# Routing for groups of batches, gates in the token table, the expert bias by matmul, a narrower maximum pass

## What is computed

```python
def _L0_ffn_ref(x, wg, W, b):
    xt = x.reshape(-1, Hv)
    logits = xt @ wg
    probs = jax.nn.softmax(logits, axis=-1)
    idx = jnp.argmax(probs, axis=-1)
    gate = jnp.take_along_axis(probs, idx[:, None], axis=1)
    onehot = jax.nn.one_hot(idx, Ev, dtype=x.dtype)
    expert_out = jnp.einsum('nh,eoh->neo', xt, W) + b[None, :, :]
    combine = onehot * gate
    out = jnp.einsum('ne,neo->no', combine, expert_out)

x = x + tanh(g_xattn[0]) * xattn(layernorm(x), ctx_2048, ctx_2048)
x = x + tanh(g_ffn[0]) * ffn(layernorm(x), wg, W, b)
```

## Time and profile before

| | us |
|---|---|
| median of 3 runs | 644.13 |
| lowest and highest | 641.44, 649.53 |
| span of the profiled execution | 645.9 |
| PE busy | 533.8 (83%) |
| DVE busy | 469.3 (73%) |
| ACT busy | 352.5 (55%) |
| POOL busy | 325.5 (50%) |

### The profile page before, as it was taken

How to read it: one execution, slowest core, us unless ns; L and a number is a source line. 1 busy time by engine, 2 the same in 40 slices (tenths; PEclk the granted TensorE clock), 3 DMA queues, 4 the chain that set the end, 5 groups by cost and what they waited for, 6 DMA issues and landing times.

```text
span 645.9 us, 10904 instructions
## 1 busy us (share of the span) xinstructions
PE 533.8 (83%) x2584; PEld 179.0 (28%) x2585; DVE 469.3 (73%) x1017; ACT 352.5 (55%) x457; POOL 325.5 (50%) x574
## 2 busy tenths in 40 slices
PE   0077989798978989999988899889999776889994
PEld 0011222222222323323222322323233133444441
DVE  5387888696878979898988989798987636323332
ACT  2112867575766677686766677686666822111110
POOL 5431536282737556474736557474434436343541
PEclk9999999798999999999999999999999978999998
DMA  4734445364647574846657575835462645543320
GB/s 131 189 105 154 116 134 148 102 151 130 131 150 179 148 171 127 195 136 159 141 142 180 145 167 146 184 113 148 104 141 42 179 132 177 117 144 96 102 79 5
DMA packets 35290, 87.80 MB, mean 136 GB/s; under 512 B 10281, under 2 KB 10430, under 8 KB 35104
## 3 DMA queue, kind: packets, MB, share of 16 engines
q1 hardware_dynamic: 26208, 62.27, 39.3%
q0 software_dynamic: 9056, 25.23, 12.1%
HBM read 64.56 MB, written 27.11 MB: 142 GB/s over the span
## 4 chain that ended last, share of the span: by engine, by line
PE 31%; DMA 18%; DVE 17%; issue 11%; POOL 9%; SPq 3%; ACT 1%; POOLq 0%; DVEq 0%
DMA stacks<-shift_parts 13%; DVE neg_max L756 11%; PE ps_scores L1238 10%; PE ps_pv L1130 7%; PE ps_ring L1099 6%; PE ps_scores L1115 4%; DMA table_dram<-token_i,dest_i 2%; SPq L343 2%; DMA prep<-recs_dram,token_cols 2%; PE ps_pv L1147 2%; POOL table_dram L523 2%; POOL prep L463 2%; DVE den L794 1%; ACT probs L672 1%; PE ps_scores L1225 1%
## 5 line engine op out<-in xcount | busy, mean ns | idle before, releaser
L756 DVE TENSOR_REDUCE neg_max<-ps_ring 128x1 f32<-128x512 f32 x512 | 335.4, 680 | 76.1 <-PE ps_ring L1099 74.1
L672 ACT ACTIVATE probs<-ps_scores 128x1024 f32<-128x1024 f32 x256 | 249.2, 1022 | 112.0 <-PE ps_scores L1115 110.8
L1099 PE MATMUL ps_ring<-stacks 128*128 128x512 bf16 x512 | 201.0, 403 | 55.3 <-DMA stacks<-zeros 30.7
L1115 PE MATMUL ps_scores<-stacks 128*128 128x512 bf16 x512 | 156.1, 388 | 20.2 <-DMA stacks<-shift_parts 19.2
L1130 PE MATMUL ps_pv<-probs,v_ones 128*32 128x512 f32 x1024 | 138.2, 612 | 0.0
L1099 PEld LDWEIGHTS ps_ring<-stacks 128*128 128x128 bf16 x512 | 49.6, 97 | 240.6 <-DVE neg_max L756 191.0
L1238 PE MATMUL ps_scores<-w_sb,probs 128*128 x184 | 87.2, 619 | 3.3 <-DVE v_ones L927 1.3
L435 POOL TENSOR_SCALAR rs<-mv 128x1 f32<-128x1 f32 x32 | 6.1, 189 | 131.7 <-DVE mv L772 89.4
L1115 PEld LDWEIGHTS ps_scores<-stacks 128*128 128x128 bf16 x512 | 48.1, 101 | 65.4 <-issue 25.2
L710 ACT COPY probs<-ps_scores 128x512 f32<-128x512 f32 x23 | 13.4, 587 | 82.2 <-PE ps_scores L1225 82.2
L927 DVE TENSOR_TENSOR v_ones<-ps_scores,stacks 128x512 f32<-128x512 f32 x23 | 15.9, 692 | 57.6 <-PE ps_scores L1238 55.2
(11 more groups left out here) (138 smaller groups left out, 481.1 us busy)
## 6 DMA issues: line engine op xcount, KB each, us to landing
parts_dram<-prep POOLq DMA_DIRECT2D x16, 768.0 KB, 7.1
stacks<-parts_dram SPq DMA_DIRECT2D x64, 192.0 KB
recs_dram<-rec SPq DMA_DIRECT2D x16, 514.0 KB, 3.9
stacks<-parts_dram SPq DMA_DIRECT2D x64, 128.0 KB
w_sb<-w_t SPq DMA_DIRECT2D x16, 512.0 KB, 9.4
prep<-x_perm SPq DMA_DIRECT2D x16, 256.0 KB, 5.2
prep<-k_perm SPq DMA_DIRECT2D x16, 256.0 KB, 8.3
v_in<-v_t SPq DMA_DIRECT2D x16, 256.0 KB, 8.9
```

The source lines that it names most:

```text
L672: nc.scalar.activation(probs[:, k % 2, 2 * jp:2 * jp + 2], ps_scores[:, jp], ACT.Exp).then_inc(exp_done, 1)
L756: nc.vector.tensor_reduce(neg_max[:, g, j, c:c + 1], ps_ring[:, u.slot(n)], AX.X, ALU.max, negate=True).then_inc(ring_free, 1)
L1099: nc.tensor.matmul(ps_ring[:, u.slot(n + c)], q_stack[0:KA, B.p, g, j, c * 128:(c + 1) * 128], k_stack[0:KA, B.p, g, j], start=True, stop= ...
L1115: last = nc.tensor.matmul(ps_scores[:, jp, j % 2], k_stack[0:KA, B.p, g, j, c * 128:(c + 1) * 128], q_stack[0:KA, B.p, g, j], start=True, ...
```

## The change

- The maximum pass reads the 96 rows with content (`KS`) instead of 128 (`KA`); `zeros` and its DMA are gone.
- Batches 2 to 7 are in the loop, 8 to 15 written out. The weights come in the first eight batches, two pieces in each.
- Logits are kept for all batches. Routing is done for groups of 8, 4, 2 and 2 batches (`GROUPS`), in batches 9, 13 and 15 and in the expert stage (`ROUTED`), with three functions on DVE and 2n matmuls on PE for a group of n. The token stores of a group, one for each batch, follow one another; those of the first group are split, four before `split_maxima(10, 0)` and four at the end of batch 9.
- A table entry has two words, token and gate; the record has lost the gate and is 1024 words. SP's record store waits for the normalized rows.
- The slot list is read in blocks of 32 entries, so that four blocks a slot land on the partitions in such a way that DVE's 32x32 transposes give the columns; PE's transposes of it are gone.
- The number of tiles is found by rounding instead of comparisons with all block ends. `turn_back` in batch 15 stands at (2, 1) as in the others.
- The bias is loaded at the start, split by POOL into three bf16 parts at the end of batch 1, and added by a bf16 matmul ahead of the slot's four f32 ones. `combine` is one instruction.
- In the expert stage the last two batches' tokens are both stored at slot 3, and the waits for the second list stand before scatter 3.

```diff
-EARLY = -(-((NB - 2) * ROWS - 127 * NE) // 128)
+GROUPS = ((0, 8), (8, 12), (12, 14), (14, 16))
+ROUTED = (9, 13, 15, None)
+EARLY = -(-(14 * ROWS - (TILE - 1) * NE) // TILE)
+PHASES = ((2, 0, EARLY), (3, EARLY, NSLOT - EARLY))
-REC = 2 * DM + 4
+REC = 2 * DM
...
-            with eng.Fori(1, 6) as i:
+            with eng.Fori(1, 4) as i:
...
-                if B.known(0) and g == 0:
-                    sp.wait_ge(pads_in, 16)
-                sp.dma_start(q_stack[KS:KS + NP, B.p, g].rearrange("p j m -> p (j m)"),
-                             zeros[:]).then_inc(stack_in[B.p][g], 16)
...
             def store_record(B):
-                sp.wait_ge(gate_ready, B.b + 1)
+                sp.wait_ge(xn2_ready, B.b + 1)
...
             def emit(B, prev, prev2, nxt, prep):
-                load_weights(B)
+                if not isinstance(B.b, int) or B.b < NB // 2:
+                    load_weights(B)
                 load_shift(B, 1)
-                if B.known(NB - 1):
-                    sp.wait_ge(scores_ready, 2 * STEPS * (NB - 1))
-                    sp.dma_start(bias_sb.rearrange("p e n -> p (e n)"), bias.partition_broadcast(128)).then_inc(bias_in, 16)
...
+            def store_tokens(first, last):
+
+                for b in range(first, last):
+                    pool.indirect_dma_start(table_dram, bass.IndirectOffsetOnAxis(ap=dest_i[:, b:b + 1], axis=0),
+                                            entries[:, b], None).then_inc(table_out, 16)
...
                 if prev:
                     rstd2(B.plus(-1))
-                if prev2 and not B.known(NB - 1):
-                    store_tokens(B.plus(-2))
-                if B.known(NB - 1):
-                    read_slots(0, EARLY, NB - 2)
-                    pool.wait_ge(rec_out[1], 16 * (NB // 2 - 1))
+                if B.known(ROUTED[0]):
+                    pool.wait_ge(table_set, 16)
+                    pool.wait_ge(dest_ready, 1)
+                    store_tokens(0, 4)
+                if B.known(ROUTED[1]):
+                    pool.wait_ge(dest_ready, 2)
+                    store_tokens(*GROUPS[1])
+                if B.known(ROUTED[2]):
+                    pool.wait_ge(dest_ready, 3)
+                    store_tokens(*GROUPS[2])
+                    read_slots(0)
+                    records_stored(GROUPS[2][1])
                     pool.wait_ge(cols_ready, 1)
-                    for r in range(NREC):
-                        gather(r, r)
+                    for s in range(NREC):
+                        gather(s)
                 if nxt:
                     split_maxima(B.plus(1), 0)
...
                 spread_sums(B, 0)
+                if B.known(ROUTED[0]):
+                    store_tokens(4, 8)
+                if B.known(1):
+                    split_bias()
...
-            store_tokens(last.plus(-1))
             for s in range(NSLOT):
-                if s == 2:
-                    store_tokens(last)
                 if s == 3:
-                    read_slots(EARLY, NSLOT - EARLY, NB)
-                scatter(s, s % NREC)
+                    pool.wait_ge(dest_ready, 4)
+                    store_tokens(*GROUPS[3])
+                    read_slots(1)
                 if s + NREC == EARLY:
                     pool.wait_ge(cols_ready, 2)
-                    for p in range(2):
-                        pool.wait_ge(rec_out[p], 16 * NB // 2)
+                    records_stored(NB)
+                scatter(s)
                 if s + NREC < NSLOT:
-                    gather(s + NREC, s % NREC)
+                    gather(s + NREC)
...
+            def find_gates(group):
+
+                of = slice(*GROUPS[group])
+                dve.wait_ge(gate_summed, group + 1)
+                chain.add(nc.vector.reduce_sum(gate_sum[:, of], gate_exp[:, of], AX.X))
+                chain.settle()
+                chain.add(nc.vector.reciprocal(gate_inv[:, of], gate_sum[:, of]))
+                chain.settle()
+                chain.add(nc.vector.tensor_scalar(entries[:, of, 1].bitcast(F32), gate_inv[:, of], gates[:, 3:4], None,
+                                                  ALU.mult))
+                chain.settle()
+                nc.vector.tensor_copy(dest_i[:, of], dest_f[:, of]).then_inc(dest_ready, 1)
...
+                        for group in range(2):
+                            if B.known(ROUTED[group]):
+                                if at == (1, 1):
+                                    find_experts(group)
+                                if at == (4, 0):
+                                    take_ranks(group, ranks_bank)
+                                if at == (5, 0):
+                                    find_gates(group)
+                        if B.known(ROUTED[2]):
+                            if at == (1, 1):
+                                find_experts(2)
+                            if at == (2, 0):
+                                take_ranks(2, ps_ring[:, 0])
+                                count_tiles(0)
+                                find_blocks(0)
+                            if at == (3, 0):
+                                find_gates(2)
+                                name_experts(0)
+                                take_tiles(0)
+                            if at == (6, 3):
+                                take_columns(0)
...
+            for s in range(NSLOT):
+                if s == 2:
+                    take_logits(last)
+                    find_experts(3)
+                if s == 3:
+                    take_ranks(3, ps_ring[:, 1])
+                    find_gates(3)
+                    count_tiles(1)
+                    find_blocks(1)
+                if s == 4:
+                    name_experts(1)
+                if s == 5:
+                    take_columns(1)
+                combine(s, ps_y[:, s % 2])
...
-                    nc.tensor.matmul(ps_ring[:, u.slot(n + c)], q_stack[0:KA, B.p, g, j, c * 128:(c + 1) * 128],
-                                     k_stack[0:KA, B.p, g, j], start=True, stop=True).then_inc(ring_full, 1)
+                    nc.tensor.matmul(ps_ring[:, u.slot(n + c)], q_stack[0:KS, B.p, g, j, c * 128:(c + 1) * 128],
+                                     k_stack[0:KS, B.p, g, j], start=True, stop=True).then_inc(ring_full, 1)
...
+                nc.tensor.matmul(bank, choose_bias[:, phase, col:col + 1].to_broadcast([128, 128]), bias_parts[:],
+                                 start=True, stop=False)
```

604 lines of the change are left out of this document (270 added, 334 removed).

## The result

| | before | changed |
|---|---|---|
| median | 646.13 us | 706.27 us |
| lowest and highest | 641.44, 649.53 | 701.99, 712.84 |
| span of the profiled execution | 645.9 | 711.2 |

The changed kernel takes 1.096 times as long, with an interval of [1.086, 1.107]: 60 us slower, where 14 were forecast. Its profiled execution is the slow one of its four (712.8 against 702.0 to 709.4 us), so differences of under 5 us against it are not read, and a larger one only where other runs show it too.

A forecast was written before the change was run, and what follows sets the result against it. It took steady batches as bound by the stack load, the shift landing 14.4 us later. Terms -7.5 + 12.4 + 12.5 + 1.3 - 0.7 = +18.0, less some 2 for shorter records, +16, gave 660 us; 8 in 10: 634 to 674.

The forecast's parts named there:

- Steady batches: Batches 0 to 14 without the bursts: lighter DVE and POOL work, weights and unrolling together give -7.5 us (-30 to +3).
- By my reading the 2.5 us are slack on POOL: Steady batches: the 2.5 us of POOL's removed casts, store and counter were not on the path.
- the landing as stack load plus 14.4 us: Steady batches: the shift rows, which start the next batch, land 14.4 us after SP issues the stack load, whatever POOL does.
- rival E: Parts and stacks late after batch 9, PE cold after each dry stretch: +10 us, 670 us; chance 0.10.
- Weights: First eight batches, 1 MB each instead of 0.5: costs 0.4 us a batch in 2 to 7, 1 us in 0 and 1 together.
- Bursts: Batches 9 and 13: POOL's gate wait and four stores delay the next shift, +5.2 and +5.9, plus 1.3: +12.4 us (6 to 18).
- the fastest landing 1.7: Bursts: the shift load issued behind the four stores lands 1.7 us after its issue.
- Batch 15 to slot 6: Longer path through stores, slot lists and gathers leaves PE dry for some 12 us: +12.5 us (+6 to +17).
- Slots 7 to 22: Expert stage: bias matmuls add 3.7 us over 16 slots, fewer record waits save 2.4: +1.3 us (-2 to +6).
- B: Rival: POOL bounds the steady batches, so ten batches gain 1.7 us more each, 17 us: 643 us; chance 0.16.
- C: Rival: back-to-back stores land together after 8 us and gates come early, bursts +6, tail +7: 648 us; chance 0.17.
- A: Main case, as summed: steady batches stay bound by the stack load, bursts and late stores cost: 660 us (652 to 672); chance 0.46.

The follow-up runs named there:

- e8: Changed kernel with only the issue of the 768 KB parts write moved to the end of POOL's batch: 665.99 us, ratio 1.030 to before.
- e14: Changed kernel with parts write last up to batch 8, behind `lows` afterwards, stores two a batch in batches 9 to 14, both list chains early, small reorderings: 633.23 us, 0.984.
- e3: Changed kernel with the weights as before, one 512 KB piece in each of 16 batches: 699.23 us, ratio 1.077 to before.
- e13: e6 with four indirect gathers of 128 x 8 bytes, read by nothing, in batch 9 where the changed kernel has its first four stores: 681.81 us, 1.060.
- e2: Changed kernel with all of `lows` and its parts write moved to the end of POOL's batch: 674.75 us, ratio 1.040 to before.
- e6: Changed kernel with POOL's wait for the gates kept ahead of the split, but the stores of groups 0 and 1 two a batch at batch ends: 675.88 us, 1.046.
- e11: Changed kernel with parts write last, stores behind `add_attention`, first slot list's stores sooner, last two batches routed one slot sooner: 641.79 us, ratio 1.003 to before.
- e1: Kernel before with only POOL's token store moved behind all other POOL work of the batch: 681.17 us, ratio 1.048.
- e12: Kernel before with only the issue of the parts write moved from behind `lows` to the end of POOL's batch: 641.85 us, ratio 1.004.
- e5: Changed kernel with e2's edit, and the token stores of groups 0 and 1 two a batch at the ends of batches 9 to 14: 673.98 us, 1.041.

## Why the prediction was wrong, and where it was right

- **Steady batches: wrong in sign** (-3 forecast for batches 2 to 8, measured +17.2). The step that failed is "By my reading the 2.5 us are slack on POOL" together with "the landing as stack load plus 14.4 us". The first asked only who waits for the freed instruction, not which DMA behind it starts sooner; the second took for a constant what depends on where the parts write lies. Batch 1, from which the constant was upheld (16.7 us), could have warned: the lag wasn't constant there either. The trace that it had also held the answer: the write of batch 1 leaves at 106.48, 7.3 us behind the stack load instead of 9.7 as in the middle batch. Removing the small work was worth something, as e8 (196.9) and e14 (197.4 against 208.0 us) show, some 1.5 us a batch, twice the 0.7 forecast; the early write cost 28 us on top of it (225.2 - 196.9).
- **PE's clock** was asked about in rival E for dry stretches only. In the changed kernel it falls at batch heads. In the first 3.49 us of batch 9, behind a wait of 3.85 us, the granted clock is 0.50, which is 1.2 instead of 2.4 GHz:

```profile
342.31 0.63 PE L1119 MATMUL ps_scores<-stacks 128*128 128x512 bf16 x1 [3.85 <-DMA stacks<-shift_parts]
```
```profile
342.31:345.80 3.49, 3.49 (x11) 1.00 (x14) 1.78 (x4) 2.05 (x2) 0.00 (x0) 0.50 0.15 58
```

  and the first pair of scores behind a long wait takes 1.03 instead of 0.60 us in the row of the middle batch above (3.97 us of wait). In the kernel before, the batches from 5 on, with waits of 0.6 to 1.6 us, kept 0.60. So a late shift can cost twice, by the wait and by slower steps behind it; how much of the 3 us each has was not measured apart.
- **Weights: not contradicted in batches 2 to 7.** 0.4 us a batch was taken, and e3 shows none that can be told there; its 12 us over the whole kernel are unexplained.
- **Bursts: mechanism half right, size wrong** (+12.4 forecast, +7.8 with the savings of the same batches; +35.4 in batches 9 to 13). POOL's wait, four issues, split and SP's issues came as summed (S + 32.4 against 31.5 us, although the gates came at S + 24.9 instead of 22.5), and e13, where nothing is written, gives 33.8 us. The failed term is "the fastest landing 1.7": with four stores unfinished it was 9.3 us, and 11.9 from the first issue until PE went on. A store's own landing stood in the earlier trace rows (7.0 to 11.4 us) and was used for the slot lists, but not for a load of another queue. In batches 10 to 12 (+9.0) the early write can be told, 78.4 us in e2 and 77.7 in e8 against 91.4 and e3's 83.8; what the burst adds there can't (e6 81.9, e3 83.8).
- **Batch 15 to slot 6: the path right, the size at the top of its range.** With the shift load of batch 15 53.3 us later, the forecast stores at 514.8 and 516.1 are 568.1 and 569.4, and the product of slot 6 ends at 630 to 637. POOL and PE in order of time:

```profile
567.57 1.07 POOL L521 DMA_INDIRECT table_dram<-entries,dest_i  x1 [0.16 <-issue]
568.95 0.97 POOL L521 DMA_INDIRECT table_dram<-entries,dest_i  x1 [0.30 <-issue]
579.96 1.05 POOL L543 DMA_INDIRECT slot_tokens<-table_dram,slot_block  x1 [10.04 <-DMA table_dram<-entries,dest_i]
```
```profile
588.17 1.09 PE L1178 MATMUL ps_scores<-identity,recs 128*128 128x128 f32 x4 [11.36 <-DMA recs<-recs_dram,token_cols]
```
```profile
631.55 1.08 PE L1178 MATMUL ps_scores<-identity,recs 128*128 128x128 f32 x4 [12.99 <-DMA recs<-recs_dram,token_cols]
...
632.86 4.52 PE L1195 MATMUL ps_scores<-w_sb,f_xt 128*128 x8
```

  The product ends at 637.4, the upper end: from the shift load of batch 15 it is 84.0 us instead of 67.8, +16.2 where +12.5 (6 to 17) was forecast. PE runs dry for 11.4 and 13.0 us, where "some 12 us" stood for both together. e11 and e14 take most of it away by order alone.
- **Slots 7 to 22: somewhat too dear.** 64.8 us for 16 slots, 4.05 each instead of the 4.29 of before, so -3.8 where +1.3 was forecast: the bias matmul costs what was said (it starts 0.21 us ahead of the product, 637.65 to 637.86), but the waits that went with it were larger than the 2.4 us allowed. The stage is now PE's without a gap, 64.59 of 64.80 us. That the rest came to +12.0 where +11.1 was forecast is luck to this extent: +16.2 and -3.8 missed their terms by 3.7 and 5.1 us in opposite directions. The 2 us for the shorter records no run shows: a gather's median landing was 4.2 us before and 4.4 after.

```profile
637.65 0.38 PE L1191 MATMUL ps_scores<-bias_parts,choose_bias 128*128 128x512 bf16 x1
637.86 3.60 PE L1195 MATMUL ps_scores<-w_sb,f_xt 128*128 x8
```

- **Rivals.** B is refuted by e1, C by batch 9's landing: the stores did not land together after 8 us but one after another, the last 13.4 us behind its issue, and nothing hides. B's 17 us were also priced too high by its own numbers: from 29.1 to 27.4 us is 1.7 for each of ten batches, and A's sum already had 7 of these 17 us. Case E had the right direction and named late parts and a cold PE, for 10 us instead of some 45. No rival held a way in which the freed time of POOL does harm.

**What stays open.** That the early parts write delays the shift is shown from both sides by e1, e2 and e8; which resource they share (the same few DMA engines, or memory) is argued, not shown. Why the kernel before gains nothing from e12 is not known, nor why its batches 2 and 3 start PE 16.2 and 16.4 us behind a stack load with the write at 9.9 and 9.7. Whether unfinished reads would hold a load back was not tested. The cost of the cold PE apart from the wait was not measured.

## What to carry to other kernels

When an edit takes work out of an engine's queue, list the DMAs which that queue issues behind it and ask what they will run into 2 us sooner; a big write may be better held back until the load that the critical engine waits for has landed or nearly so (here 7.2 us behind the stack load did harm, 12 us and more did none). Small scattered writes are not done when they are issued: a load issued behind them, here on another queue, can land as late as they do, so issue the load first or keep such stores away from it, a few at a time. A burst that is cheap by its issue times should be costed by its landing times.

## What the runs showed of the hardware that was not expected

- A 4 KB load of one queue landed 9.3 us after its issue behind four unfinished 128 x 8 byte stores of another queue, 1.7 us behind four gathers of the same size, which were all but done when it was issued, and 4.2 us where it was issued ahead of the stores.
- The four stores, issued 1.3 us apart, landed 6.7, 9.7, 12.4 and 13.4 us behind their issues, one after another, and the load 0.7 us behind the last.
- The other way round, two such stores issued 1.3 us behind a 768 KB write of the same queue went with a landing of that write after 15.4 instead of 9.7 us (e5).
- Moving one token store of each batch behind POOL's other work, which lets a 768 KB write leave 2.5 us sooner, made the kernel 31 us slower (e1).
- A wait of PE of 3.85 us at a batch's head was followed by 3.5 us at a granted clock of 0.50, though such waits didn't always do it: in the kernel before a wait of 3.12 us was followed by 0.50 (116.0 to 119.5), one of 3.00 us by 1.00 (180.95 to 184.4), and in e1 one of 4.05 us left the first pair at 0.60 us.
